# Row-max steps of the next attention head issued six steps ahead of the score chunks instead of eight

## The reference

```
xn = layernorm(x)                                  # x: (2, 2048, 256)
z  = layernorm(xn) * ln1_g + ln1_b
q, _, v = split(z @ w_in.T + b_in);  k = q         # 16 heads of 16 columns
scores = einsum('nhld,nhsd->nhls', q, k) / sqrt(16)
attn = softmax(scores)                             # over 2048 columns of each row
a = einsum('nhls,nhsd->nhld', attn, v) @ w_out.T + b_out
f = gelu(xn @ ternary(W1).T + b1) @ ternary(W2).T + b2
out = x + a + f
```

## Time and profile before

| what | value |
|---|---|
| median of 3 runs | 1436.96 us (1436.22 to 1437.12) |
| the profiled execution | 1435.52 us |
| its span in the profile | 1433.7 us |
| PE, DVE, ACT, POOL busy | 97%, 93%, 87%, 8% |
| one head in the middle, DVE's row-max to row-max | 36.37 us |

### The profile page before, as it was taken

How to read it: one execution, slowest core, us unless ns; L and a number is a source line. 1 busy time by engine, 2 the same in 40 slices (tenths; PEclk the granted TensorE clock), 3 DMA queues, 4 the chain that set the end, 5 groups by cost and what they waited for, 6 DMA issues and landing times.

```text
span 1433.7 us, 32248 instructions
## 1 busy us (share of the span) xinstructions
PE 1384.6 (97%) x13414; PEld 447.5 (31%) x13414; DVE 1339.1 (93%) x1430; ACT 1247.3 (87%) x2284; POOL 113.7 (8%) x246
## 2 busy tenths in 40 slices
PE   7899987999999999999999999999999999999999
PEld 5666542222222222222222222222222222222244
DVE  7868779999999999999999999999999999999934
ACT  5554643999999999999999999899999999999975
POOL 2000005000000000000000000000222200002200
PEclk8999999999999999999999999999999999999999
DMA  6012000010000000100000001001212101001122
GB/s 232 16 36 76 30 16 1 28 31 30 31 31 31 30 31 30 31 30 26 29 30 29 32 29 33 28 32 35 60 61 61 61 31 33 32 33 60 39 100 81
DMA packets 28531, 60.69 MB, mean 42 GB/s; under 512 B 6200, under 2 KB 11736, under 8 KB 28130
## 3 DMA queue, kind: packets, MB, share of 16 engines
q1 hardware_dynamic: 27810, 56.99, 11.8%
q10 hardware_dynamic: 576, 1.65, 0.3%
HBM read 41.29 MB, written 16.77 MB: 40 GB/s over the span
## 4 chain that ended last, share of the span: by engine, by line
DVE 71%; PE 23%; ACT 2%; DMA 2%; issue 1%; POOL 0%; SPq 0%; ACTq 0%; DVEq 0%
DVE part_max L839 68%; PE ps L367 6%; PE ps L384 3%; PE ps L1070 3%; PE ps L1139 3%; PE ps L330 2%; PE ps L1085 2%; PE ps L458 1%; DVE w L831 1%; ACT w L1020 1%; DMA rows<-in_rows 1%; PE ps L439 1%; ACT hidden L1015 1%; PE ps L1111 1%; ACT w L1049 1%
## 5 line engine op out<-in xcount | busy, mean ns | idle before, releaser
L1049 ACT ACTIVATE w<-ps 128x512 f32<-128x512 f32 x2048 | 1111.4, 596 | 63.8 <-PE ps L384 21.6
L839 DVE TENSOR_REDUCE part_max<-ps 128x1 f32<-128x1024 f32 x1024 | 1164.8, 1211 | 1.9 <-PE ps L330 1.7
L367 PE MATMUL ps<-w,v_ones 128*32 128x256 f32 (+1 forms) x7688 | 628.6, 399 | 0.4
L384 PE MATMUL ps<-qry,key 50*128 50x512 f16 x1984 | 411.4, 388 | 7.2 <-ACT w L1049 7.0
L330 PE MATMUL ps<-qry,key 48*128 48x512 f16 x2048 | 404.2, 380 | 11.4 <-DVE part_max L839 11.3
L367 PEld LDWEIGHTS ps<-w,v_ones 128*32 128x32 f32 x7688 | 152.2, 108 | 384.7 <-issue 211.5
L384 PEld LDWEIGHTS ps<-qry,key 50*128 50x128 f16 x1984 | 101.1, 93 | 440.7 <-ACT w L1049 412.5
L330 PEld LDWEIGHTS ps<-qry,key 48*128 48x128 f16 x2048 | 101.5, 95 | 36.8 <-DVE part_max L839 26.4
L638 POOL COPY v_ones<-v_all 128x128 f32<-128x128 f32 x64 | 18.6, 291 | 743.9 <-PE ps L367 743.9
L1011 ACT ACTIVATE q_split<-ps,sigma_bq 128x512 f16<-128x512 f32 x16 | 11.0, 687 | 65.2 <-PE ps L1085 65.2
L1070 PE MATMUL ps<-w_ternary,w 128*128 128x256 f16 x512 | 61.7, 277 | 6.2 <-DVE w L831 6.2
(11 more groups left out here) (144 smaller groups left out, 466.2 us busy)
## 6 DMA issues: line engine op xcount, KB each, us to landing
key<-q_parts SPq DMA_DIRECT2D x64, 128.0 KB
qry<-q_parts SPq DMA_DIRECT2D x64, 128.0 KB
o_heads<-o_evacuated SPq DMA_DIRECT2D x31, 256.0 KB, 10.2
resid<-in_x SPq DMA_DIRECT2D x8, 512.0 KB, 13.8
q_parts<-q_split SPq DMA_DIRECT2D x16, 256.0 KB, 2.5
key<-q_parts SPq DMA_DIRECT2D x64, 64.0 KB
qry<-q_parts SPq DMA_DIRECT2D x64, 64.0 KB
out<-resid SPq DMA_DIRECT2D x7, 512.0 KB, 3.1
```

The costliest lines, as they stand in the source:

```text
L367: mm = eng.matmul(pv[32 * c:32 * c + 2 * D, c0:c1], vst[:, kb, :], prob[kb % 2][:, c * BANK + c0:c * BANK + c1], start=(kb == 0), stop=(kb ...
L384: eng.matmul(ring_bank(v, i, False), key[v][r:r + KROWS, kb * P:(kb + 1) * P], qry[v][r:r + KROWS, c * BANK:(c + 1) * BANK], start=True, s ...
L839: dve.tensor_reduce(part_max[h % 2][:, a // 2, a % 2:a % 2 + 1], pa[a % 2], AX.X, ALU.max).then_inc(s_r, 1)
L1049: act.activation(prob[kb % 2][:, c * BANK:(c + 1) * BANK], ring_bank(k, i, last), ACT.Exp, scale=exp_scale).then_inc(s_e, 1)
```

## The change

The number of steps by which pass A runs ahead goes from 8 (2 periods of 4 steps) to 6. Slots 0 to 25 of a head now carry steps 6 to 31 of head h+1, and slots 26 to 31 carry steps 0 to 5 of head h+2. The loop ahead of the first head issues steps 2 to 5 instead of 2 to 7. The transposition stays at the start of slot 28. DVE, ACT, POOL and SP run the same instructions in the same order.

```diff
-AHEAD = 2
+LEAD = 6
 STEPS = 4
...
-                steps = iter([(1 if q + AHEAD < NPER else 2, STEPS * ((q + AHEAD) % NPER) + n) for n in range(STEPS)])
+                steps = iter([(1 + (STEPS * q + n + LEAD) // NA, (STEPS * q + n + LEAD) % NA) for n in range(STEPS)])
...
-            for a in range(2, STEPS * AHEAD):
+            for a in range(2, LEAD):
                 a_step(pe, 1, 1, a)
```

## The result

The changed kernel is slower: 1460.54 us at the median (1454.58 to 1461.04, four runs) against 1436.59 (1436.21 to 1437.12, four runs). The ratio is 1.0157, with a 95% interval of 1.013 to 1.0184. The profiled execution took 1460.15 us, its span is 1458.3 instead of 1433.7. So 24.6 us have to be found.

A forecast was written before the change was run, and what follows sets the result against it. DVE's reductions were taken to bound the kernel. Waits 18.3, head starts 5.4, reciprocals 2.3 and ends -1.7 made +24.3 on 1435.52, so 1459.8; the timed median lies 1.44 higher, hence 1461 us, range 1450 to 1479.

The forecast's parts named there:

- What bounds the kernel; the margin: DVE sets a head's length; PE reaches the transposition 0.97 us after its data, while the change delays the data 2.26 us.
- The wait in each head: At slot 28, PE waits for the transposition's data and DVE idles 0.61 us per head: 18.3 us over 30 heads.
- rival 4: Behind the transposition, ACT's lag still holds the second chunk, without clock trouble: about 1475 us, chance 5%.
- The head's start: At the late step after the whole value product, DVE idles 0.17 to 0.18 us more in 30 heads: 5.4 us.
- The ordinary heads together: The transposition's wait and the late step after the value product, over 30 heads: 18.3 + 5.4 us.
- The two reciprocals: Right before step 0 in two places, they lengthen PE's wait and half clock follows: 0.8 and 1.5, together +2.3 us.
- The ends: Behind the last fold, the last transposition follows its neg_max sooner, so less stands behind DVE's train: -1.7 us.
- N: The time at which neg_max starts; the transposition was predicted at N + 1.02 and DVE's next step at N + 1.83.
- the start: Around the first heads: the first chunk no longer waits for two of head 1's steps; no time in the sum.
- The transposition doesn't wait long enough: At slot 28 the wait is too short to reach DVE, only the gain behind the last fold counts: 1435 us, chance 3%.
- no difference: The wait costs DVE only some 0.05 us per head, which the 1.7 behind the last fold gives back: 1437, chance 3%.
- The clock rival: PE falls to half clock behind the transposition in ordinary heads, 1.5 us each: 1483 (half) or 1506 (all), chance 14%.

The follow-up runs named there:

- e10: The kernel before (lead of 8) with three unused POOL operations between neg_max and the split: 1437.38 us, ratio 1.0007.
- e9: The changed kernel (lead of 6) with three unused POOL operations between neg_max and the split: 1503.54 us, ratio 1.0446.
- e1: The changed kernel with a lead of 7 instead of 6, transposition still in slot 28: 1434.87 us, ratio 1.0.
- e2: The changed kernel with its transposition one slot later, ahead of chunk 58, lead still 6: 1434.48 us, ratio 0.9992.
- e3: The kernel before with its transposition two slots earlier, ahead of chunk 52, lead of 8 kept: 1462.30 us, ratio 1.0174.
- e4: The changed kernel with DVE's fold one reduction earlier, right behind a head's last row-max step: 1433.92 us, ratio 0.9987.
- e11: The changed kernel with a lead of 7 and three unused POOL operations between neg_max and the split: 1443.05 us, ratio 1.0053.
- e5: The changed kernel with a lead of 5 instead of 6, transposition still in slot 28: 1540.84 us, ratio 1.0736.
- e6: The changed kernel with its transposition two slots later, ahead of chunk 60: 1452.62 us, ratio 1.0123.
- e7: The changed kernel with a lead of 5, the fold right behind the last row-max step, transposition ahead of chunk 58: 1435.58 us, ratio 0.9994.

## Why the prediction was right

The time was forecast as 1461 us and came out as 1460.54. Step by step:

*What bounds the kernel; the margin.* Right. DVE's train of reductions sets the head, and PE's place for the transposition had 0.97 us to spare against 2.26 of delay. e10 takes 0.54 of that margin (by the heads of e9) without a loss, e1 uses it up without a loss, and e2, e3 and e4 each move the distance at a fixed lead and move the time by some 26 us and a head by 0.73 to 0.75 (36.40 in e2 and 36.42 in e4 against 37.15; 37.10 in e3 against 36.37).

*The wait in each head.* Right in mechanism and size: 0.59 instead of 0.61. The handover from POOL to PE, which no row of before showed, is 0.05 (POOL ends at 754.57, the weight load starts at 754.62); I took 0.07. That ACT would have emptied its ring is shown by ACT's idle 0.90 before its copy, so nothing held the second chunk back, and rival 4 didn't happen. e11 tests the threshold: with two reductions to do in the meantime the longer chain leaves next to nothing at the fold.

*The head's start.* Right: 0.18 more (0.26 instead of 0.08), as predicted. e11 shows it by itself: a head 0.18 longer than in e1 (36.56 and 36.38), nearly all of it in the bracket at the head's start.

*The ordinary heads together.* 37.15 - 36.37 = 0.78 in 30 heads, 23.4 us. The prediction had 18.3 + 5.4 = 23.7.

*The two reciprocals.* Together 24.8 - 23.4 = 1.4 against 2.3, and the split was wrong: beyond what ordinary heads cost, the two heads around the first take 1.5 us more than before (78.56 instead of 75.52, less 2 x 0.78), where 0.8 was predicted, and those around the second nothing (75.09 instead of 73.49, less 2 x 0.78), where 1.5 was. At the first PE idled 2.57 us (2.6 predicted), the clock fell for longer than I had assumed, and DVE waited four times (0.99, 0.76, 0.76 and 0.33). The windows show half clock over all of 944 to 948:

```profile
943.25 1.23 DVE L839 TENSOR_REDUCE part_max<-ps 128x1 f32<-128x1024 f32 x1 [0.99 <-PE ps L330]
945.23 1.23 DVE L839 TENSOR_REDUCE part_max<-ps 128x1 f32<-128x1024 f32 x1 [0.76 <-PE ps L330]
947.21 1.22 DVE L839 TENSOR_REDUCE part_max<-ps 128x1 f32<-128x1024 f32 x1 [0.76 <-PE ps L330]
...
944.00:948.00 4.00, 4.00 (x28) 0.67 (x24) 2.49 (x3) 2.17 (x4) 0.00 (x0) 0.50 0.01 3
```

At the second the step "above the 1.38 that was followed by the drop, so 1.5" failed. PE idled 1.77 us there and the clock stayed at 1.00:

```profile
1242.60 0.23 PE L351 MATMUL ps<-ident_f,max_split 128*32 128x128 f16 x1 [1.77 <-POOL max_split L648]
...
1242.00:1246.00 4.00, 3.40 (x37) 0.91 (x37) 3.49 (x4) 3.04 (x7) 0.46 (x3) 1.00 0.03 6
```

*The ends.* The gain behind the last fold is 2.0 instead of 1.7. The 0.3 between them can't be told from the scatter: in e10, where the last transposition stands at N + 2.71 as before, this part took 70.72, 0.4 less than before.

What I priced at nothing is the start: between the folds of head 0 and head 1 the changed kernel takes 1.6 us more. DVE's rows there, first before, then changed, then e2:

```profile
245.11 23.84 DVE L839 TENSOR_REDUCE part_max<-ps 128x1 f32<-128x1024 f32 x21 [0.85 <-PE ps L330]
...
233.25 0.75 DVE L759 SCALAR_TENSOR_TENSOR resid<-ps,hidden_unscale,resid 128x512 f32<-128x512 f32 x1 [0.64 <-PE ps L1070]
...
244.32 1.22 DVE L839 TENSOR_REDUCE part_max<-ps 128x1 f32<-128x1024 f32 x1 [1.27 <-PE ps L330]
245.80 24.98 DVE L839 TENSOR_REDUCE part_max<-ps 128x1 f32<-128x1024 f32 x22 [0.25 <-PE ps L330]
...
243.04 1.23 DVE L839 TENSOR_REDUCE part_max<-ps 128x1 f32<-128x1024 f32 x1 [1.27 <-PE ps L330]
244.67 24.98 DVE L839 TENSOR_REDUCE part_max<-ps 128x1 f32<-128x1024 f32 x22 [0.41 <-PE ps L330]
```

The 0.64 comes behind a stretch at half clock that the profile of before hasn't (nor has any of the eleven experiments' profiles):

```profile
228.00:231.30 3.30, 3.30 (x15) 1.08 (x14) 3.27 (x4) 0.00 (x0) 0.90 (x4) 0.50 0.00 0
```

PE's programs are the same to the row up to 233.15, so this part is not the change's but an accident of the execution. The other part, 0.9 us, goes with the lead. All profiles run the first chunks at half clock for a while. Where that lasts some 7 us and there is no earlier stretch, the time from fold to fold is 39.03 at a lead of 8 (before and e10), 39.48 at 7 (e1 and e11) and 39.96 and 39.98 at 6 (e2 and e9). So giving up a step of lead does cost something by itself, some 0.46 us, but once in the execution and not in every head. The half clock has its part in that: in e5, with a lead of only 5, it lasts some 3.4 us and the time is 39.12. What makes it shorter there the runs don't show.

In the profile, this miss (1.8 with the 0.2 ahead of the fold of head 0) nearly cancels the 0.9 of the reciprocals, the 0.3 of the ordinary heads and the 0.3 behind the last fold: +24.3 predicted, +24.6 measured. And the four timed runs themselves lie between 1454.58, at a mean granted clock of 0.993, and 1461.04, the other three at 0.988. So the last tenth of a per cent of the agreement is luck.

*The rivals.* "The transposition doesn't wait long enough" and "no difference" were out by the same rows as the forecast. The clock rival did not come at 0.97 us of idle PE, but it was real and near: half a us more (e9) brought it, at the 1.5 us per fall that the prediction had worked out from one episode.

## What to carry to other kernels

When a step is moved in an in-order queue, look for the fixed wait whose producer moves with it, and compare the shift (here 2.26 us) with the margin that the wait had (0.97). What then reaches the bounding engine isn't the wait's length but the chain from the producer to the next piece of work, less the work that the engine still has queued. Moving the producer (e4) or the waiting instruction (e2) along with the change loses nothing in ordinary heads that a time can tell. Whether it keeps the small gain at the ends is at the edge of what the runs can tell (e4: 0.9987, 0.9975 to 0.9998; e2: 0.9992, 0.9983 to 1.0002). Such a wait has two sides, though: two slots too late and the transfers behind it become the wait (e6).

## What the runs showed of the hardware that I had not expected

The length of one idle gap of PE doesn't tell whether the granted clock falls behind it. It fell after 1.38 us (kernel before, first reciprocal) and stayed up after 1.77 (changed kernel, second reciprocal). Behind a gap of 1.45 at the first reciprocal it stayed at 1.00 in e4 and was at 0.63 from 925 to 928 in e7. In e9 the gap is 1.51 in each of two heads: the clock was at 0.59 behind the one at 740.56 and at 1.00 in the windows behind the one at 1132.11. Executions of one kernel differ in it too: e9's run of 1486.79 us had a mean granted clock of 0.982, its three of 1501 to 1508 us one of 0.966 to 0.970. A fall costs this kernel 1.5 us, and more where the clock stays down longer (heads of 41.0 in e5, 2.8 more). In e5 that came to nearly as much as the waits that had caused it, in e9 to more than the three POOL operations themselves: of e5's 105 us, about 57 are the wait's (30 heads of 38.28 instead of 36.37) and most of the rest is the clock's.
